# Degree count of a graph layer: one-hots of a group in two VectorE operations, three staircases instead of four

## The reference

```
deg  = segment_sum(ones_like(src), dst, num_segments=N)
dinv = rsqrt(maximum(deg, 1e-12))
coef = (dinv[src] * dinv[dst])[:, None]
xw   = x @ Wg
gcn  = segment_sum(xw[src] * coef, dst, num_segments=N) + bg
```

## Time and profile before

| | us |
|---|---|
| median of 3 runs | 1596.47 |
| lowest to highest | 1595.73 to 1596.88 |
| profiled execution, its own time | 1599.57 |
| profiled execution, its span (first to last instruction) | 1597.8 |
| stage with the degree count, from TensorE's first transpose in the loop to the one behind its last group | 20.66 to 186.92 |

### The profile page before, as it was taken

One profiled execution on the slowest core, in us unless ns is written; L12 is line 12 of the kernel. 1 busy time (PEld: TensorE's weight loads), 2 busy tenths in 40 slices (PEclk: granted clock), 3 DMA queues, 4 the chain that ended last, 5 costly groups with the idle time before them and its releaser, 6 DMA issues.

```text
span 1597.8 us, 25329 instructions
## 1 busy us (share of the span) xinstructions
PE 1499.5 (94%) x7913; PEld 944.2 (59%) x7913; DVE 1093.2 (68%) x3316; ACT 605.9 (38%) x1382; POOL 919.1 (58%) x1026
## 2 busy tenths in 40 slices
PE   5788899999999998999998999998999999999995
PEld 3566678766666664444443444445777777777763
DVE  6899766767777775544445444447788878888775
ACT  5999876633333222111111111112333333333332
POOL 0000000047777776677776777776777777777772
PEclk9999999999999998899999999999999999999997
DMA  6444444489999998889988899888999999999894
GB/s 232 139 159 159 167 142 156 151 289 306 331 315 315 333 300 266 281 289 288 295 281 264 287 289 307 291 271 276 297 297 314 299 299 292 311 299 305 283 301 134
DMA packets 172759, 423.89 MB, mean 265 GB/s; under 512 B 24142, under 2 KB 25802, under 8 KB 172616
## 3 DMA queue, kind: packets, MB, share of 16 engines
q0 software_dynamic: 71120, 236.74, 46.7%
q1 hardware_dynamic: 79980, 146.16, 27.0%
q10 hardware_dynamic: 21516, 39.29, 6.5%
HBM read 351.42 MB, written 70.67 MB: 264 GB/s over the span
## 4 chain that ended last, share of the span: by engine, by line
PE 73%; DVE 12%; DMA 6%; ACT 5%; issue 2%; POOL 0%; SPq 0%; DVEq 0%; ACTq 0%
PE bank L1343 15%; PE bank L1344 15%; PE bank L1345 15%; PE bank L1464 12%; PE bank L1466 11%; DVE stage L973 3%; DMA scaled_g<-pairs 2%; DMA gathered<-scaled_g,index_slots 2%; DVE stage L969 2%; DVE operands L982 2%; PE bank L1595 1%; ACT pairs L628 1%; ACT operands L613 1%; ACT stage L634 1%; DMA combine<-values 1%
## 5 line engine op out<-in xcount | busy, mean ns | idle before, releaser
L562 POOL DMA_INDIRECT gathered<-scaled_g,index_slots x882 | 878.2, 996 | 310.7 <-issue 187.4
L1089 DVE TENSOR_SCALAR one_hot<-iota_bf,dst_in_tile,gathered 128x128 bf16<-128x128 bf16 x882 | 270.9, 329 | 315.9 <-DMA gathered<-scaled_g,index_slots 290.9
L1343 PE MATMUL bank<-weights,operands 128*128 128x512 f32 x784 | 396.5, 506 | 7.4 <-DVE stage L989 4.0
L1464 PE MATMUL bank<-gathered,one_hot 128*128 128x512 f16 x882 | 344.7, 391 | 26.0 <-DVE one_hot L1089 25.8
L1466 PE MATMUL bank<-gathered,one_hot 128*128 128x512 f16 x882 | 339.9, 385 | 0.0
L1344 PE MATMUL bank<-weights,operands 128*128 128x512 f32 x784 | 311.6, 397 | 0.0
L1345 PE MATMUL bank<-weights,operands 128*128 128x512 f32 x784 | 311.0, 397 | 0.0
L547 POOL COPY dst_slots<-dst_cols 128x18 f32 x49 | 14.7, 300 | 332.0 <-issue 330.2
L732 ACT ACTIVATE operands_f<-operands,cos_sin_v 128x512 f16<-128x512 f32 x98 | 69.8, 720 | 335.7 <-PE bank L1345 239.4
L1343 PEld LDWEIGHTS bank<-weights,operands 128*128 128x128 f32 x784 | 149.5, 191 | 71.7 <-DVE stage L989 6.5
L1464 PEld LDWEIGHTS bank<-gathered,one_hot 128*128 128x128 bf16 x882 | 86.0, 98 | 170.4 <-issue 76.8
(11 more groups left out here) (240 smaller groups left out, 2090.3 us busy)
## 6 DMA issues: line engine op xcount, KB each, us to landing
operands<-values SPq DMA_DIRECT2D x98, 256.0 KB, 5.5
stage<-in_x SPq DMA_DIRECT2D x96, 256.0 KB, 2.8
turned_x<-operands SPq DMA_DIRECT2D x37, 512.0 KB, 3.3
operands<-turned_x SPq DMA_DIRECT2D x37, 512.0 KB, 6.4
gathered<-scaled_g,index_slots POOLq DMA_INDIRECT x882, 5.2
scaled_g<-pairs SPq DMA_DIRECT2D x49, 260.0 KB, 2.1
pairs<-scaled_g SPq DMA_DIRECT2D x49, 260.0 KB, 4.4
values<-stage ACTq DMA_DIRECT2D x49, 256.0 KB, 4.3
```

Source lines behind the costliest of these rows:

```text
L562: pool.indirect_dma_start(out=plain(row_ring[k % RING]), out_offset=None, in_=table, in_offset=bass.IndirectOffsetOnAxis(ap=index_slots[:, ...
L1089: dve.tensor_scalar(one_hot[:, k % HOT, :], iota_bf[:, :], column(dst_in_tile, seq % 2 * PER_TILE + k), scale_of(row), ALU.is_equal, ALU.m ...
L1343: pe.matmul(out_ap, a_hi, b_hi, start=start and n == 0, stop=False, skip_group_check=True)
L1464: pe.matmul(gcn_banks[seq % 2][:, :], one_hot[:, k % HOT, :], hi, start=k == 0, stop=False, skip_group_check=True)
```

## The change

`STAIRS` goes from 4 to 3, so VectorE writes six one-hots of dst mod 128 in each group instead of five. VectorE writes a group in two operations instead of six: the one of dst div 128 as before, but 50 wide, and one for all six columns of dst mod 128 (768 elements). For this the columns are held as 16-bit values written twice in a row (`dst_div2`, `dst_mod2`), and each comparison walks over pairs: two neighbouring numbers of `iota_bf` against the two equal copies. The pair is then read again for the next two numbers. The copies are made by `repeat_columns`, for the first 81 columns before the loop, for the other 815 after tile 0's groups. They lie in `pairs`, which is free until the node table is made. TensorE's order stays as it is; the matmul of the sixth column now adds to the one-hot side of bank 5.

```diff
-    GROUP, STAIRS = 9, 4
+    GROUP, STAIRS = 9, 3
...
-        dst_div = extra_row[:, :].bitcast(BF16)[:, 0:COLS]
+        twice_room = pairs[:, :, :].rearrange("p a d -> p (a d)")
+        dst_mod2, dst_div2 = (twice_room[:, n * COLS:(n + 1) * COLS].bitcast(BF16).rearrange("p (c two) -> p c two", two=2)
+                              for n in range(2))
...
-            link(dve.tensor_copy(dst_div, div_i))
+
+            def repeat_columns(a, b):
+                link(dve.tensor_copy(dst_div2[:, a:b, :], div_i[:, a:b].unsqueeze(2).to_broadcast([P, b - a, 2])))
+                link(dve.tensor_copy(dst_mod2[:, a:b, :], mod_i[:, a:b].unsqueeze(2).to_broadcast([P, b - a, 2])))
+
+            repeat_columns(0, 9 * GROUP)
...
+                if t == 0:
+                    repeat_columns(9 * GROUP, COLS)
...
-                dve.tensor_tensor(div_hot[half][:, :, 0:TILES],
-                                  iota_bf[:, 0:TILES].unsqueeze(1).to_broadcast([P, GROUP, TILES]),
-                                  dst_div[:, c0:c0 + GROUP].unsqueeze(2).to_broadcast([P, GROUP, TILES]), ALU.is_equal)
-                for c in range(HOTS):
-                    last = dve.tensor_scalar(mod_hot[half][:, c, :], iota_bf[:, :], column(dst_mod, c0 + c), None,
-                                             ALU.is_equal)
+                for hot, twice, count, width in ((div_hot[half], dst_div2, GROUP, DIVW), (mod_hot[half], dst_mod2, HOTS, P)):
+                    shape = [P, count, width // 2, 2]
+                    last = dve.tensor_tensor(
+                        hot[:, 0:count, :].rearrange("p c (j two) -> p c j two", two=2),
+                        iota_bf[:, 0:width].rearrange("p (j two) -> p j two", two=2).unsqueeze(1).to_broadcast(shape),
+                        twice[:, c0:c0 + count, :].unsqueeze(2).to_broadcast(shape), ALU.is_equal)
```

## The result

| | before | after |
|---|---|---|
| median of 4 runs, us | 1596.68 | 1569.9 |
| lowest to highest | 1595.73 to 1598.17 | 1569.08 to 1570.12 |
| profiled execution: its own time, its span | 1599.57, 1597.8 | 1570.04, 1568.2 |
| stage with the degree count | 166.3 | 138.8 |

The ratio is 0.9831, with a 95% interval of 0.9813 to 0.9848: 26.8 us less, where 28.7 were forecast. The stage with the degree count became 27.4 us shorter in the profiled execution. In two later comparisons it took 138.6 and 138.9 us.

The account below looks back on a forecast made before the run. VectorE was taken to bound the degree-count stage from about tile 9, ScalarE before. Wins of 0.6 (tiles 0 and 1), 6.2 (2 to 8) and 21.9 us (9 to 30) make 28.7: 1596.47 to 1567.8, range 1563 to 1573.

Parts of the forecast that it names:

- The bound: Degree-count stage: VectorE sets the pace from about tile 9 on, ScalarE ahead of that.
- The group: VectorE's packed group at two elements per cycle: pitches 0.30 and 0.47, 0.77 us where 1.35 stood.
- The pace: Tiles 9 to 30: a loop through three engines of 4.33 us, starting 0.2 earlier; 4.15 taken per tile.
- the sum: Degree-count stage: 0.6 us won in tiles 0 and 1, 6.2 in 2 to 8, 21.9 in 9 to 30; 28.7 together.
- the first part: Loop through three engines, from the end of one tile's products to the next tile's last group: 4.33 us forecast.
- The early tiles: Tiles 2 to 8, set by ScalarE: three stairs less in each, 7 x 3 x 0.293 = 6.2 us won.
- The first two tiles: Tiles 0 and 1: the win covers the cost of the added casts, and 0.6 us is left.
- The wait behind the casts: Behind tile 0's third group, two casts at 3.7 us together make TensorE wait 1.5 us instead of 0.34.
- rival 3: Later stages give the gain back: time stays within 3 us of 1596.5; chance 0.03.
- Rival 1: VectorE's pair isn't taken at two per cycle: a group costs 1.41, 5 us slower, 1601.5; chance 0.08.
- Rival 2: Two per cycle only in part; first price: group 1.01, 20 us won, 1577; second: 11 us won, 1585; chance 0.13.
- the table of the Trainium skill: Sources not delivering two neighbouring words at a time take about 1.7 times as long: group 1.2, 10 us won, 1586.

Follow-up runs that it names:

- the second comparison: The changed kernel, not altered further, run again against the kernel before: 31.1 us less, ratio 0.9826, stage 138.6 us.
- the long wait above: TensorE's 4.83 us wait in the changed kernel with the two 1630-element casts done twice: 16.5 us below the kernel before (one run), stage 144.2.

## Why the prediction was right

**The bound.** VectorE's rows set the late tiles and ScalarE's the early ones, as read. With three staircases and nothing packed the late tiles grew by what VectorE got more to do; with the packing and four staircases ScalarE became full at 4.47, and the early tiles stayed as they were.

**The group.** 0.77 us was the forecast of a packed group. The chain of the kernel with one unpaired comparison has the packed one of 768 elements at 0.47 to 0.48, as forecast, and the durations of 387 and 551 ns are within 10 ns of the forecast. In the changed kernel two groups take 1.54 us, from 103.68 to the next operation at 105.22, which is 0.77 each. The step from "all operands move on by one 16-bit element" to "two per cycle" was the one that rested on a bound and not on a row; the unpaired kernel, with the same elements, types and number of operations, shows that the gain hangs on the pair.

**The pace.** 4.15 was taken for the late tiles, from a loop through three engines; 4.16 came (159.66 - 68.06 = 91.60 over 22 tiles). 21.6 us were won there, where the sum had 21.9. That a loop through three engines holds the tiles, two staircases show (4.08, and no wait), and the unpaired smaller comparison, whose chain runs through it. But the prediction closed the loop in each tile: 4.33 less the 0.2 by which the last group stands behind the products. It closes over two tiles. Where the first part measured 4.75, closing it in each tile would give 4.55; the tiles took 8.77 / 2 = 4.38. For the change itself the two ways happen to agree, 4.13 and 8.31 / 2 = 4.16, so part of the match of 4.15 and 4.16 is luck.

**The early tiles.** The sum had 6.2 us for tiles 2 to 8 and they won 5.35 (40.67 to 35.32). Here a term was too large: it took three staircases off each of the seven tiles. Five of them did so, by 0.86 to 0.88 us each (7.00 to 6.13, 5.22 to 4.34). Tile 2 won 0.42; with the casts in pieces it took 4.34 instead of 4.81, so the missing part was the casts'. Tile 7 won 0.56 (6.07 to 5.51): its chain runs through all three engines and ends in the seven transposes of the edge sources (0.80 us), which are TensorE's.

**The first two tiles.** 0.6 us forecast, 0.5 won. The wait behind the casts was forecast at 1.5 us. In the profile after it is 0.66, and 1.65 in the second comparison. The difference is tile 0, which took 6.84 and 5.62 us in the two: TensorE begins the loop with products 0.43 us apart, as behind the long wait above, and goes over to 0.23 at 26.6 us in the one and 23.6 in the other. The profile's clock row reads 1.00 there all the same, so that this is the lower level again is likely and not shown. A later change of pace hides more of the casts, so the sum of the two tiles is nearly the same, 11.9 and 11.7.

**The rest.** 0.5 + 5.35 + 21.55 = 27.4 in the stage, 26.8 between the medians. The block behind the stage slid forward as a whole within what the times can tell, and rival 3 had no part. Between the profiled executions it is 29.5, since that of before lay 3 us above its own median; the prediction had set that aside.

**The rivals.** Rival 1 needed the unpaired form, and with it the kernel is slower: 8.1 us, and 6.2 in the stage, where it had said 5. Rival 2's first price, 20 us won, was 18.9 in the stage (166.3 - 147.4) when its condition was made true. The 10 us that it took from the table of the Trainium skill did not come up in any run.

## What to carry to other kernels

A broadcast value that is compared with a 16-bit tensor can be held twice in a row and read as a pair that stands still on the next step: that alone took a two-tensor operation from 1.04 to 0.52 ns per element, and made one large operation (a pitch of 0.47 us) cheaper than six small ones with a scalar each. Where two engines stand close behind each other as a stage's bound, work has to leave both in one step: here one half of the change won 16 us, the other lost 9, and both won 27. When every engine's own list is shorter than the pace, look for the loop through all of them, count over how many tiles it closes, and shorten what stands in it: here 0.46 us in the loop cost 0.23 per tile. Work that is not in the loop costs nothing until its engine is full.

## What was not expected of the hardware

TensorE's clock has a price of its own for a wait: behind 4.83 us without a matmul it was granted 0.50 in the windows from 34 to 39 us, behind 1.65 us it stayed at 1.00. A cast whose source repeats each 32-bit element took 1.04 ns per element with an odd number of columns (1850 ns for 815 columns, 322 for 81) and 0.52 to 0.54 with an even one (363 ns for 194 columns), where the cast of the same types without a repeat took 0.53.
